# Fewer waits at ScalarE's state stores, and one load in place of eight for the counts that SyncE waits for

## The reference, cut to what matters

```python
zs, zd = ZU[:, src, :], ZU[:, dst, :]                 # ZU = Z projected by U: 4 heads x 16
logits = (zs * zd).sum(-1) / scale
seg_max = segment_max(logits, dst)
exp_l = exp(logits - seg_max[:, dst])
alpha = exp_l / (segment_sum(exp_l, dst)[:, dst] + 1e-16)
agg = segment_sum(alpha[..., None] * zs, dst)         # per destination node
ssa = einsum('k,knr,kdr->nd', w, agg, U)              # then Z_half, residual, relu
x = layernorm(x + layer0(x)); x = layernorm(x + layer1(x))
```

## Time and profile before

| | us |
|---|---|
| median of three runs | 3666.26 |
| the profiled execution, its own time | 3677.74 |
| its span (first to last instruction) | 3675.2 |
| PE busy | 1971.2 (54%) |
| DVE busy | 1919.5 (52%) |
| POOL busy | 1728.5 (47%) |
| ACT busy | 1168.6 (32%) |

### The profile page before, as it was taken

The page is one execution under the profiler, slowest core; times in us unless marked ns, Lnnn a source line. Parts: engine busy times, 40 slices in busy tenths (PEclk is TensorE's granted clock), DMA queues, the critical chain, the costliest instruction groups (busy, mean ns, idle before and its releaser), DMA issues. The chain is left out here.

```text
span 3675.2 us, 61713 instructions
## 1 busy us (share of the span) xinstructions
PE 1971.2 (54%) x15251; PEld 1490.8 (41%) x15252; DVE 1919.5 (52%) x5864; ACT 1168.6 (32%) x3040; POOL 1728.5 (47%) x1832
## 2 busy tenths in 40 slices
PE   9345545454545445454545455464545454567776
PEld 9233333343434334343424243343433333444666
DVE  4444646454545546454545455464545454666477
ACT  1112323222232323322232233233232322334477
POOL 1544454445444444554544544445544444252662
PEclk7555555555555555555555555555555555577798
DMA  6212222121212212121212112121212121285343
GB/s 205 52 32 46 47 44 46 42 46 42 48 41 47 46 41 48 42 49 40 47 39 48 42 44 48 41 50 41 48 40 45 41 49 39 58 274 179 112 140 107
DMA packets 406593, 232.96 MB, mean 63 GB/s; under 512 B 284096, under 2 KB 371434, under 8 KB 406506
## 3 DMA queue, kind: packets, MB, share of 16 engines
q1 hardware_dynamic: 346666, 154.11, 15.4%
q0 software_dynamic: 59840, 77.87, 9.8%
HBM read 134.80 MB, written 42.55 MB: 48 GB/s over the span
## 5 line engine op out<-in xcount | busy, mean ns | idle before, releaser
L576 POOL DMA_INDIRECT arena<-z_table,sslot x1563 | 1492.0, 955 | 1646.2 <-SPq L418 1114.0
L1347 PE MATMUL bank<-arena 128*128 x4992 | 613.8, 222 | 637.7 <-issue 585.8
L1347 PEld LDWEIGHTS bank<-arena 128*128 128x128 bf16 x4992 | 457.5, 105 | 789.5 <-issue 697.0
L1584 ACT ACTIVATE arena<-bank 128x272 f32<-128x272 f32 x416 | 269.8, 661 | 1574.8 <-remote 970.4
L902 DVE TENSOR_TENSOR xin<-arena,bank 128x512 f32<-128x512 f32 x208 | 143.1, 688 | 1044.3 <-remote 588.2
L1561 ACT ACTIVATE acc<-xTb 128x68 f32 x1600 | 384.6, 312 | 306.6 <-issue 296.0
L1364 PE MATMUL bank<-xto,arena 128*128 128x68 bf16 x3328 | 321.6, 246 | 147.5 <-issue 147.4
L1335 PE MATMUL bank<-ident_b,arena 128*128 128x128 bf16 x1664 | 214.8, 310 | 339.4 <-remote 205.3
L1364 PE MATMUL bank<-arena 128*128 128x68 bf16 x1664 | 296.9, 243 | 120.2 <-issue 90.5
L1364 PEld LDWEIGHTS bank<-xto,arena 128*128 128x128 bf16 x3328 | 281.5, 132 | 166.9 <-issue 166.9
L1335 PEld LDWEIGHTS bank<-ident_b,arena 128*128 128x128 bf16 x1664 | 160.4, 141 | 399.6 <-remote 200.2
(11 more groups left out here) (264 smaller groups left out, 2543.6 us busy)
## 6 DMA issues: line engine op xcount, KB each, us to landing
arena<-arena SPq DMA_DIRECT2D x1660, 32.0 KB
arena<-z_table,sslot POOLq DMA_INDIRECT x1563
dspace<-in_xT SPq DMA_DIRECT2D x49, 256.0 KB
xmz_table<-agn SPq DMA_DIRECT2D x49, 256.0 KB
xmz_table<-arena SPq DMA_DIRECT2D x14, 896.0 KB
arena<-in_x SPq DMA_DIRECT2D x13, 896.0 KB, 11.4
out<-arena SPq DMA_DIRECT2D x12, 896.0 KB
xin<-in_xT SPq DMA_DIRECT2D x8, 896.0 KB
```

Source lines behind the costliest of these rows:

```text
L576: pool.indirect_dma_start(ring[:, e % RING, :], None, z_table, bass.IndirectOffsetOnAxis(ap=sslot[:, e:e + 1], axis=0)).then_inc(tiles_in[ ...
L1347: last = T.matmul(zd_ps[g % 2][:, u * KR:(u + 1) * KR], onehotT[:, g * G + u, :], z3[:, bass.ds(tiles[u], 1), s, :].rearrange("p a c -> p ...
L1584: A.activation(sums[:, :, 1 + q * Q:1 + (q + 1) * Q].rearrange("p c j -> p j c"), sum_ps[q % 2][:, 0:Q * AW].rearrange("p (j c) -> p j c", ...
```

## The change

SyncE: a new function `load_needs` loads all eight counts of a block with one instruction at the head of the block, and `copy_steps` takes its two from there. ScalarE: in `store_states` the wait stands at every fourth state only, and there for all stores before it.

```diff
+            def load_needs(b):
+
+                _, need = nc.values_load_multi_w_load_instructions(
+                    needs[0:1, bass.ds(b * NG * 2, 2 * NG)], engines=[mybir.EngineType.SP], min_val=16 * G, max_val=16 * G * EG)
+                return need
+
-            def copy_steps(b, h, g, uses):
+            def copy_steps(b, h, g, uses, need):
...
-                    need = [sp.value_load(needs[0:1, bass.ds((b * NG + g) * 2 + i, 1)], min_val=16 * G, max_val=16 * G * EG) for i in range(2)]
                     for i in range(2):
-                        sp.wait_ge(tiles_in[i], need[i])
+                        sp.wait_ge(tiles_in[i], need[2 * g + i])
...
             def turn(b, h, uses, store, load):
 
+                need = load_needs(b)
                 for g in range(2):
-                    copy_steps(b, h, g, uses)
+                    copy_steps(b, h, g, uses, need)
...
-                    if u >= NSPARE:
-
-                        act.wait_ge(state_stored, B * b + u - NSPARE + 1)
+                    if u >= NSPARE and u % NSPARE == 0:
+
+                        act.wait_ge(state_stored, B * b + u)
```

More of the change, by code:

```diff
@@ L445, in _ @@
             sp.wait_ge(dloc_ready, 1)
+            need = load_needs(0)
             for g in range(2):
-                copy_steps(0, 0, g, 1)
+                copy_steps(0, 0, g, 1, need)
             sp.wait_ge(reset_ready, 1)
@@ L474, in turn @@
                 for g in range(2, NG):
-                    copy_steps(b, h, g, uses)
+                    copy_steps(b, h, g, uses, need)
             for g in range(2, NG):
-                copy_steps(0, 0, g, 1)
+                copy_steps(0, 0, g, 1, need)
             sp.wait_ge(prep_read, 6)
             load_tiles(0, 0)
+            need = load_needs(1)
             for g in range(NG):
-                copy_steps(1, 1, g, 1)
+                copy_steps(1, 1, g, 1, need)
             with nc.sync.Fori(1, NB // 2 - 2) as i:
```

## The result

The changed kernel takes 3893.85 us (median of four runs, 3889.14 to 3911.84), the kernel before beside it 3670.22: a ratio of 1.062, interval 1.057 to 1.067. It is slower by 224 us, and the forecast of 3622 with its range up to 3725 was wrong. The profiled execution of after took 3911.84 us of its own time, with a span of 3910.0.

The account below looks back on a forecast made before the run. A block was taken as a cycle bound by slow stretches that follow GpSimd's gather runs, with no engine full. Terms of -1.3 + 0.9 - 0.5 + 0 = -0.9 us over 49 blocks gave -44 us: 3622, range 3560 to 3725.

Parts of the forecast that it names:

- What bounds the kernel: Whole block: a cycle of 58.8 us on average; no engine is full, and slow stretches follow GpSimd's gather runs.
- In front of g2: SyncE before g2's copies: eight instructions gone, so g2 and the last product come 1.3 us sooner a block; bounds 0.9 to 7.1.
- whatever moves g2 moves the rest: From g2's first copy to VectorE's last product: a stiff distance, 29.2 us in one block and 30.6 in another.
- In front of g0: SyncE before g0: eight instructions go, eighteen come; g0, GpSimd's second run and x_ready 0.9 us later; bounds 0 to 10.
- the rival: GpSimd's second run of 8 gathers grows to 16 ahead of x_ready, VectorE stands: 3750 or 3707 us; chance 0.22.
- In front of g1: SyncE before g1: eight instructions fewer, one or two more copies escape the second stretch; 0.5 us off a block, bounds 0 to 6.
- ScalarE: ScalarE's state stores: dearer waits and fewer instructions, both hidden until x_ready; 0 taken, bounds -3 to +2.2 us a block.
- The sum: All terms a block: -1.3 + 0.9 - 0.5 + 0 = -0.9 us, times 49 blocks, -44 us.
- the larger gain: Rival: slow stretches are shared, so half of 8 x 1.0 us before g2 counts, -3 us a block: 3520; chance 0.11.

Follow-up runs that it names:

- e5: Changed kernel, with g0's ring-space token to GpSimd held until x_ready of the block before (count b): 3613.43 us, ratio 0.980.
- e6: Changed kernel, with g1 alone loading and checking its own two counts as before the change: 3647.47 us, ratio 0.990.
- e9: Kernel before, with only g0's ring-space token held until x_ready has its count for block b-1: 3672.73 us, against 3691.51 for the kernel before.
- e10: Changed kernel with g0's token held until the block before has ended, the same code as e5, measured again: 3622.0 us, against 3691.51 for the kernel before.
- e12: Changed kernel, with g1 and g3 each loading and checking their own two counts as before: 3656 us, against 3691.51 for the kernel before.
- e11: Changed kernel, with g3 alone loading and checking its own two counts as before: 20 us above an expected 3860 to 3910 us.
- e2: Kernel before with ScalarE's part of the change alone (a wait at every fourth store): 3676.11 us, ratio 0.998.
- e1: Kernel before with SyncE's part of the change alone (one load of eight counts), old ScalarE waits: 3907.35 us, ratio 1.065.
- e7: Kernel before with each gather fetching 16 rows in place of 128, the number of gathers kept: 3669.47 us, beside 3697.84.
- e8: Kernel before, with a small GpSimd memset and a wait for it between two gathers of a group: 3893.4 us, ratio 1.053.
- e4: Changed kernel with eight no-operations of SyncE in front of the copies of g0 and of g1: 3907.96 us, ratio 1.062.

## Why the prediction was wrong

**What bounds the kernel: right.** Blocks as a cycle, slow stretches that follow GpSimd's runs, the chain that waits out the second of them. e5 and e6 move the time by 280 and 246 us through the length of the second run alone.

**In front of g2: right in sign, small.** 1.3 us were taken, and the eight instructions do take 1.32 us in the median (in front of g1, in the kernel before). With runs kept apart g2 comes 12.8 - 10.5 = 2.3 us sooner (e9, e10) and 12.4 - 10.6 = 1.8 in e12. Of the 2.3, 0.8 reaches the last product (42.2 and 41.4), so "whatever moves g2 moves the rest" was too stiff. From g2 to the last product is 31.0 us in the median of after and 29.3 before, within the 29 to 31 foretold. The 5.2 us by which g2 comes sooner in after are for the larger part the third run that is no longer there behind line 1020, and so a gift of the joined run: in e10, without joined runs, it is 12.4 - 10.5 = 1.9.

**In front of g0: wrong, and the argument against the rival rested on it.** I took 0.9 us of delay for the lump of eighteen instructions. g0 starts 1.9 us ahead of the last product where it was 0.2 ahead, and at +0.1 to -0.8 in e6, e10, e11 and e12: the lump is done inside the stretch, the lower bound of its range. But e11 shows that the place of g0 doesn't decide; the second run moves along with it.

**In front of g1: the step that failed.** "Eight instructions fewer, 1.3 us, ... so one or two copies more escape it", counted as a gain of 0.5 us. Two things were wrong.

Its size: the eight instructions are worth 1.3 us, but from g0 to g1 it is 2.4 us less (8.6 to 6.2), because a slow stretch sets in some microseconds after its run has started and also caught what stood just ahead of g1's copies; and g1's own copies take 7.9 us in the median and not 9.7. From the start of the second run, g1 is out 12.37 - 8.13 = 4.2 us sooner. (Against the last product it is 17.6 - 10.8 = 6.8, but part of that is g0, and the run moves along with g0.)

Its sign: the eighth gather ends 9.7 us after the run's start. The token behind g1 came 2.6 us after that end and now comes 1.6 us ahead of it, so the run goes on to 16 and the chain waits it out. What was summed as a small gain is a threshold with a large loss behind it.

The rival named this mechanism, with "if g1 is done some 3.5 us sooner" as its point and 1.3 to 5 us as the saving, and got 0.22. The saving was 4.2 and the threshold 2.6, both inside the bounds of 0 to 6 that I gave the step, so the rival should have weighed more. Its argument against itself, that g0 and the second run with it would be later, is no argument, since the token of g0 races that same run. It was also too rare and too cheap. Joined runs in a quarter to a half of the pairs of blocks were expected; 39 of 49 chains are long. Its price, 6 us less 2 or 3 for the block behind, was read from a single block. Inside the trace of after the long chains last 28.5 us in the mean and the others 18.4, and the last product of the block behind comes 1.4 us sooner: 8.7 us net (blocks 2 to 49, and only nine short chains). 39 - 7 = 32 more long chains are then 278 us, less the 51 that the change saves without the race: 227, where 224 were measured. From after to e10 it is 272 us for 36 chains, 7.5 each, so the price is known to about 1 us, and that the sum comes so near is partly luck.

**ScalarE: right.** 0 taken, 0.998 (0.994 to 1.002) measured in e2; its stores' busy time is 394.3 us against 384.6, but e1 with the old waits has 394.8, so not even that rise is the waits'.

**The sum: near the mark for a kernel that was not measured, and partly by luck.** -0.9 us a block x 49 = -44 us was the forecast; with the race taken out of both kernels it is -51. The terms are others, though: of the 1.3 us in front of g2 0.8 reach the last product, the 0.9 us of delay in front of g0 is not there, and the chain is 0.3 us shorter (18.6 and 18.3), where 0.5 was taken for g1.

**A slip in the larger gain.** Half of the 8 x 1.0 us in front of g2 is 4 us a block and not 3, which gives 3666 - 196 = 3470 in place of 3520.

What stays open is why a series of gather instructions slows the other engines' instruction streams at all. That the number of rows is not the cause is shown (e7), and that 0.12 us more from gather to gather does not end it (e8); a gather instruction of more than one row per partition, which would halve their number, was not tried.

## What to carry to other kernels

Where an engine hands out work in portions, the time at which a portion is handed over is a race, and a faster issuer can lose it: ask for each handover what is still running when it comes earlier, and price both sides of that threshold and not the slope beside it. When the bounds of a step reach past a rival's threshold, work out from the rows where in those bounds it lies before giving the rival its chance. If work that was late by accident protected a chain, make the order explicit with a wait (here the token behind the block's end), and the saving can then be kept.

## What the runs showed of the hardware

- GpSimd's indirect DMA costs nearly the same for 16 rows as for 128: 837 and some 950 ns of issue, and a slow stretch of the other engines comes with the small ones too, one matmul in 12 us (e7).
- SyncE's eight instructions for two counts (two loads into registers, their checks and register work) take 1.32 us in the median, as their median durations and gaps add up to the earlier trace rows. Taking them out brings the next group of DMAs 2.4 us nearer (8.6 to 6.2), the rest being time that the slow stretch had added. Eight no-operations in the same place leave no record in the trace and cost nothing that shows (e4).
- A slow stretch does not begin with its run. Over 33 runs of 16 in the kernel before, TensorE starts 10 matmuls a microsecond in the first 4 us of the run, 4.7 from 4 to 6 us, and 0.3 to 0.6 from then until about 2 us behind the run's end. So g1's copies, started 0.2 us after the run's first gather, took 7.95 us for eight, and 11.05 when started 2.1 us after it, where 5.1 us is their time undisturbed.
